# Query roots per batch on GpSimd, and the last feed-forward by halves

## The reference, cut to what matters

```python
q = (hidden @ Wq + bq).reshape(b, s, 16, 128).transpose(0, 2, 1, 3)
q = q * rsqrt(mean(q * q, -1) + 1e-6)      # the query norm; k likewise
scores = einsum('bhsd,bhed->bhse', q, k) / sqrt(128)
x = layernorm(x + (softmax(scores) @ v) @ Wo)
# gated feed-forward; _qdot casts both operands to fp8 and gives bf16
x = layernorm(x + _qdot(gelu(_qdot(x, w_gating[0])) * _qdot(x, w_gating[1]), w_linear))
```

## Time and profile before

| | |
|---|---|
| median of 3 runs | 837.78 us (837.47 to 840.25) |
| profiled execution | 837.24 us |
| span of its instructions | 835.2 us |
| mean granted clock of TensorE | 0.996 |
| PE busy | 796.5 us (95%) |
| DVE busy | 650.1 us (78%) |
| ACT busy | 528.7 us (63%) |
| POOL busy | 335.6 us (40%) |
| chain that ended last | PE 76%, DVE 10%, ACT 7%, issue 2%, POOL 2% |

### The profile page before, as it was taken

The page is one execution under the profiler, slowest core; times in us unless marked ns, Lnnn a source line. Parts: engine busy times, 40 slices in busy tenths (PEclk is TensorE's granted clock), DMA queues, the critical chain, the costliest instruction groups (busy, mean ns, idle before and its releaser), DMA issues.

```text
span 835.2 us, 13794 instructions
## 1 busy us (share of the span) xinstructions
PE 796.5 (95%) x4554; PEld 610.9 (73%) x4554; DVE 650.1 (78%) x1696; ACT 528.7 (63%) x1315; POOL 335.6 (40%) x419
## 2 busy tenths in 40 slices
PE   6899998899999999999999999999999999999985
PEld 5564576688878777886788767887788778777763
DVE  1678778798889787988878987898879877755655
ACT  3776732773664697538863598359854588578763
POOL 0686875354256213632525313723543242112110
PEclk9999999999999999999999999999999999999998
DMA  9977311001003000200100010100110001000000
GB/s 323 344 250 249 91 64 26 0 14 26 1 2 86 4 2 0 77 0 2 38 13 17 10 60 8 62 1 0 40 51 1 1 1 51 1 13 2 1 13 25
DMA packets 40517, 41.20 MB, mean 49 GB/s; under 512 B 19072, under 2 KB 34944, under 8 KB 40064
## 3 DMA queue, kind: packets, MB, share of 16 engines
q1 hardware_dynamic: 40448, 40.33, 15.2%
HBM read 31.93 MB, written 8.39 MB: 48 GB/s over the span
## 4 chain that ended last, share of the span: by engine, by line
PE 76%; DVE 10%; ACT 7%; issue 2%; POOL 2%; DMA 1%; SPq 0%; POOLq 0%; DVEq 0%; ACTq 0%
PE bank L1376 11%; PE bank L1337 10%; PE bank L1103 6%; PE bank L1160 6%; PE bank L1355 6%; PE bank L1365 5%; PE bank L1297 5%; PE bank L1230 3%; PE bank L1161 3%; PE bank L1190 3%; PE bank L1360 3%; PE bank L1097 2%; PE bank L1343 2%; PE bank L1243 2%; PE bank L1204 2%
## 5 line engine op out<-in xcount | busy, mean ns | idle before, releaser
L1337 PE MATMUL bank<-XTE,w_xq 128*128 128x256 f32 x512 | 122.0, 381 | 2.6 <-ACT QA L721 2.1
L729 ACT ACTIVATE S<-S,mx 128x128 f32<-128x128 f32 x256 | 99.4, 394 | 28.3 <-DVE mx L1034 28.0
L1376 PE MATMUL bank<-w_xo,OX 128*128 128x256 f32 x512 | 115.9, 379 | 0.0
L1337 PEld LDWEIGHTS bank<-XTE,w_xq 128*128 128x128 f32 x512 | 94.4, 190 | 20.4 <-issue 4.3
L1376 PEld LDWEIGHTS bank<-w_xo,OX 128*128 128x128 f32 x512 | 95.3, 190 | 12.2 <-issue 0.2
L1031 DVE SCALAR_TENSOR_TENSOR S<-bank,rq,xmask 128x128 f32<-128x128 f32 x256 | 71.6, 342 | 23.9 <-PE bank L1355 19.9
L720 ACT ACTIVATE QS<-bank,per_partition_sb 128x256 f32<-128x256 f32 x128 | 60.9, 475 | 28.4 <-PE bank L1337 28.2
L1160 PE MATMUL bank<-prod,taps_sb 128*128 128x256 f32 x256 | 77.6, 385 | 0.3 <-DVE Zc L846 0.3
L1355 PEld LDWEIGHTS bank<-KTX,QA 128*128 128x128 f32 x512 | 62.7, 191 | 11.5 <-issue 7.5
L1355 PE MATMUL bank<-KTX,QA 128*128 128x128 f32 x512 | 67.8, 279 | 2.2 <-ACT QA L721 1.7
L315 POOL TENSOR_TENSOR prod<-XTA,ccolA 128x256 f32<-128x256 f32 x96 | 59.1, 648 | 25.4 <-DVE prod L315 14.4
(11 more groups left out here) (230 smaller groups left out, 1744.3 us busy)
## 6 DMA issues: line engine op xcount, KB each, us to landing
keys_spilled<-KTX SPq DMA_DIRECT2D x6, 512.0 KB, 2.9
values_spilled<-VX SPq DMA_DIRECT2D x6, 512.0 KB, 4.1
KTX<-keys_spilled SPq DMA_DIRECT2D x6, 512.0 KB, 3.8
VX<-values_spilled SPq DMA_DIRECT2D x6, 512.0 KB, 4.7
xin<-in_x SPq DMA_DIRECT2D x8, 256.0 KB, 3.0
taps_sb<-in_taps SPq DMA_DIRECT2D x1, 2048.0 KB, 13.4
cnat<-in_ctx SPq DMA_DIRECT2D x8, 256.0 KB, 2.8
ccolA<-in_ctxT SPq DMA_DIRECT2D x32, 64.0 KB, 2.7
```

Source lines behind the costliest of these rows:

```text
L729: ins = nc.scalar.activation(S[:, b, seq(h)], S[:, b, seq(h)], ACT.Exp, bias=mx[:, b, h:h + 1], accum_out=sm[:, b, h:h + 1])
L1337: ins = nc.tensor.matmul(cols(EQ)[:, h], w_xq[:, k, hh * XDIM:(hh + 1) * XDIM], XTE[:, k], start=k == 0, stop=k == HALVES - 1)
L1376: ins = nc.tensor.matmul(rows(EY)[:, b], OX[:, h, b], w_xo[:, n * XGROUP + h], start=n == 0 and h == 0 and b == 0, stop=n == XKV - 1 and h ...
```

## The change

Two things. POOL's `queries` calls `inverse_root` once for each batch, on four columns, with a signal for each; DVE's `scores` of batch b waits for the signal of its own batch. And group 7's feed-forward becomes a program of its own, `last_ffn`: gelu, product, transposes, cast to fp8 and the last matmuls go by halves of 512 columns, with the results in other banks; DVE takes one of the four gate copies; and the norm's output of group 6 moves on DVE from before group 7's value copies to after its last product. The strings of PE, DVE and ACT get 2, 3 and 1 more letters a at their ends; POOL's is unchanged.

```diff
 # gpsimd, queries
-                sig(inverse_root(rq[:, n % 2], sums, XDIM * 1e-6, vq[:, n % 2]), "e_rq")
+                for b in range(GB):
+                    part = slice(b * XGROUP, (b + 1) * XGROUP)
+                    sig(inverse_root(rq[:, n % 2, part], sums[:, part], XDIM * 1e-6, vq[:, n % 2, part]), "e_rq")
 # vector, queries and scores
-                    dve.wait_ge(sems["e_rq"], g * XKV + n)
+                    dve.wait_ge(sems["e_rq"], GB * (g * XKV + n))
-                    dve.wait_ge(sems["e_rq"], nth(g, XKV, n))
+                    dve.wait_ge(sems["e_rq"], nth(g, GB * XKV, GB * n + b))
 # scalar, last_ffn
+                def gate(j):
+                    half = G16[:, j // 2, j % 2 * BANK:(j % 2 + 1) * BANK]
+                    if j < 3:
+                        act.wait_ge(sems["f_gf"], nth(g, 2 * GB, j))
+                        sig(nc.scalar.activation(half, ffn_banks(g, j)[0][:], ACT.Copy), "f_g16")
+                    act.wait_ge(sems["f_g16"], nth(g, 2 * GB, j))
+                    sig(nc.scalar.activation(half, half, ACT.Gelu_apprx_tanh), "f_ga")
+
+                def turned(j):
+                    b, nh = j // 2, j % 2
+                    act.wait_ge(sems["f_aT"], last_half(j))
+                    settled(act)
+                    sig(nc.scalar.activation(A8T[:, b, 4 * nh:4 * nh + 4].rearrange("p k s -> p (k s)"),
+                                             as_bf(ffn_banks(g, j)[0])[:, 0:BANK], ACT.Copy, saturate=False), "f_a8")
...
+                for j in range(3):
+                    yield
+                    gate(j)
+                yield
+                turned(0)
+                yield
+                gate(3)
+                for j in range(1, 4):
+                    yield
+                    turned(j)
 # vector: ffn writes its norm only for groups below 6; last_ffn
+                for j in range(2):
+                    yield
+                    value(j)
+                yield
+                product(0)
+                yield
+                value(2)
+                yield
+                product(1)
+                yield
+                dve.wait_ge(sems["f_gf"], nth(g, 2 * GB, 3))
+                dve.wait_ge(sems["f_g16"], nth(g, 2 * GB, 2))
+                sig(nc.vector.tensor_copy(G16[:, 1, BANK:2 * BANK], ffn_banks(g, 3)[0][:]), "f_g16")
+                yield
+                value(3)
+                for j in range(2, 4):
+                    yield
+                    product(j)
+                yield
+                normalised(g - 1)
...
 # tensor, last_ffn: the gating matmuls are those of ffn
+                def turned(j):
+                    b, nh = j // 2, j % 2
+                    pe.wait_ge(sems["f_a"], last_half(j))
+                    for k in range(4):
+                        ins = nc.tensor.transpose(as_bf(ffn_banks(g, j)[0])[:, seq(k)], G16[:, b, seq(4 * nh + k)], ident_bf[:])
+                    sig(ins, "f_aT")
+
+                def result(b):
+                    for nh in range(2):
+                        pe.wait_ge(sems["f_a8"], last_half(2 * b + nh))
+                        settled(pe)
+                        for k in range(4 * nh, 4 * nh + 4):
+                            ins = nc.tensor.matmul(ffn_banks(g, 2 * b)[1][:, 0:DIM], A8T[:, b, k], w_ln[:, k], start=k == 0, stop=k == FFN_K - 1)
+                    sig(ins, "f_y")
+                for j in range(3):
+                    yield
+                    turned(j)
+                yield
+                result(0)
+                yield
+                turned(3)
+                yield
+                result(1)
```

More of the change, by code:

```diff
@@ L263, in station_a @@
                     yield from ffn(g - AHEAD + 1)
-            for g in range(GROUPS - AHEAD + 1, GROUPS):
+            for g in range(GROUPS - AHEAD + 1, GROUPS - 1):
                 yield from ffn(g)
+            yield from last_ffn(GROUPS - 1)
         def each_group(program):
@@ L631, in ffn @@
                     sig(nc.scalar.activation(half, ffn_banks(g, j)[0][:], ACT.Copy), "f_g16")
[L632 to L636, removed]
                 yield
-                for b in range(GB if g < GROUPS - 1 else 0):
+                for b in range(GB):
                     act.wait_ge(sems["f_g16"], nth(g, 2 * GB, 2 * b + 1))
@@ L878, in ffn, with normalised, last_ffn, value @@
                     sig(nc.vector.tensor_tensor(UA[:, b], x[:, b], Y16[:, b], ALU.add), "f_yu")
-                    if g == GROUPS - 1 and b == 0:
+                dve.wait_ge(sems["f_yu"], nth(g, GB, GB - 1))
+                norm("f", UA)
+                if g < GROUPS - 2:
+                    yield
+                    normalised(g)
+            def normalised(g):
+                dve.wait_ge(sems["nf_rstd"], nth(g))
+                norm_out("f", UA, X[g % XBUF])
+            def last_ffn(g):
+                x = X[g % XBUF]
+                def value(j):
+                    dve.wait_ge(sems["f_gf"], nth(g, 2 * GB, j))
+                    sig(nc.vector.tensor_copy(F16[:, j // 2, j % 2 * BANK:(j % 2 + 1) * BANK], ffn_banks(g, j)[1][:]), "f_f16")
+                def product(j):
+                    half = G16[:, j // 2, j % 2 * BANK:(j % 2 + 1) * BANK]
+                    dve.wait_ge(sems["f_f16"], nth(g, 2 * GB, j))
+                    dve.wait_ge(sems["f_ga"], last_half(j))
+                    sig(nc.vector.tensor_tensor(half, half, F16[:, j // 2, j % 2 * BANK:(j % 2 + 1) * BANK], ALU.mult), "f_a")
+                for j in range(2):
[18 more added lines that the diff above has]
+                normalised(g - 1)
+                for b in range(GB):
+                    yield
+                    dve.wait_ge(sems["f_y"], nth(g, GB, b))
+                    order(nc.vector.tensor_copy(Y16[:, b], ffn_banks(g, 2 * b)[1][:, 0:DIM]))
+                    sig(nc.vector.tensor_tensor(UA[:, b], x[:, b], Y16[:, b], ALU.add), "f_yu")
+                    if b == 0:
                         dve.wait_ge(sems["f_yu"], nth(g, GB, 0))
@@ L882, in ffn @@
                 dve.wait_ge(sems["f_yu"], nth(g, GB, GB - 1))
[L883 removed]
+                norm("f", UA, GB - 1)
                 yield
[L885 to L886 removed]
+                normalised(g)
             def ternary_ffn(g):
@@ L1049, in output @@
                 norm_out("e", UE, x)
-            together(ORDER["dve"], s=set_up(), a=station_a(front, ffn), c=station_c(ternary_ffn, recurrent), r=recurrent(0), k=station_k(keys, no_turning), q=station_q(queries),
+            together(ORDER["dve"], s=set_up(), a=station_a(front, ffn, last_ffn), c=station_c(ternary_ffn, recurrent), r=recurrent(0), k=station_k(keys, no_turning), q=station_q(queries),
                      x=each_group(lambda g: scores(g, 0)), y=each_group(lambda g: scores(g, 1)), o=each_group(output))
@@ L1205, in ffn, with last_ffn @@
                     sig(ins, "f_y")
+            def last_ffn(g):
+                yield from ffn(g)
+                def turned(j):
[14 more added lines that the diff above has]
+                    turned(j)
+                yield
+                result(0)
+                yield
+                turned(3)
+                yield
+                result(1)
             def ternary_ffn(g):
```

23 lines of the change are left out of this document (16 added, 7 removed).

## The result

The kernel after takes 841.70 us (median of 6 runs, 840.48 to 843.9), the kernel before 837.62 beside it on the same chip (6 runs, 836.9 to 840.25): a ratio of 1.0053, 95% interval 1.0041 to 1.0065. It is slower by 4.1 us by the medians, by 4.4 by the ratio (3.4 to 5.4). The forecast was 839.6 us with a range up to 841.5; the sign is right, the size is less than half of what came, and the time lies outside the range.

The account below looks back on a forecast made before the run. TensorE was taken to bound most of 200 to 800 us, a chain of waits the end after 808. Profiled 837.24 + 2.63 of stalls - 0.8 = 839.1, on the median 839.6 us; range 836.8 to 841.5, forecast's own 838.4 to 840.8.

Parts of the forecast that it names:

- 155, 411 and 741: DVE's waits at 154.98, 411.30 and 741.04: earlier or later roots there change nothing for TensorE, each priced at 0.
- The tail: Last feed-forward by halves: DVE reads the last result at 828.0 instead of 828.79, 0.8 us gained, bounds 0.2 and 1.2.
- rival (a): Query roots on POOL: four columns cost what eight cost, 6.9 us slower in all, 844.7 us; chance 0.06.
- The queue behind the other roots: POOL's queue behind roots not listed: users come later than 0.8 us or a gap comes first, so no stall.
- at 375: DVE waits for batch 1's root at 368.86; the chain to X, which TensorE turns at 374.87, stalls 0.73 us.
- At 258: Four POOL products behind the root, used by TensorE at 258.56: 0.82 late less 0.06 slack, 0.76 us stall.
- At 450: POOL products ended at 450.00, used by TensorE at 450.40: 0.82 late less 0.40 slack, 0.42 us stall.
- At 183: DVE's convolution products behind batch 1's root, taken by TensorE at 183.02: 0.82 less 0.10 slack, 0.72 us stall.
- (b): Delays priced at 0, at 741.04 and 411.30, reach TensorE too: 2 x 0.8 us more, 841.2 us; chance 0.15.
- (c): Stalls in the middle of the run get absorbed, only the last feed-forward's gain is left: 837.0 us; chance 0.25.
- (d): Last feed-forward gives nothing, since DVE with its thirteen steps becomes the bound: 840.4 us; chance 0.06.
- (e): The clock: a fall of the clock costs 1.3 us; chance 0.06.

Follow-up runs that it names:

- the roots alone: Kernel before with the split roots but its old last feed-forward: 843.57 us, ratio 1.0074 to the kernel before.
- the tail alone: Kernel after with the whole roots of before, so only the new last feed-forward is changed: 836.14 us, ratio 0.9984 to the kernel before.
- the queue alone: Kernel before, roots whole, plus an unused four-column addition and power on POOL behind each root: 845.40 us, ratio 1.0096 to the kernel before.
- the norm first: Whole roots and new last feed-forward, but DVE writes group 6's norm ahead of group 7's value copies again: 836.50 us, ratio 0.9995 to before.
- the addition on VectorE by halves: Whole-root kernel with new last feed-forward, changed: DVE adds the root's small constant, POOL takes the power per batch, four columns twice: 839.4 us, ratio 1.0035 to before.
- the run without the addition: Whole roots and new last feed-forward, but query roots omit adding the small constant, leaving out part of the computation: 833.03 us, ratio 0.9958 to before.

## Why the prediction missed, step by step

**Right.** A root of four columns: forecast 1.04 on a straight line between two and eight columns, measured 1.038. POOL's extra: some 25 us, measured 25.4. That the trace is to be read by who stands directly behind a root, that the stalls add where TensorE is the bound (5.85 in the trace, 6.2 in the time), and that three places swallow theirs: 155, 411 and 741 came as said. The tail: 0.94 gained in the trace (1.26 between traces without a fall of the clock there) and 1.3 us by the ratio (0.3 to 2.3), where 0.8 was forecast. For the power the rows say about 0.4 us fixed and 0.16 us a column (0.72, 1.04, 1.67 for two, four, eight), so rival (a) is dead. The Trainium skill (GPSIMD Engine Reference, section 3.1) gives about 2.6 cycles an element for an addition of two tensors, and 4497 ns for 2048 elements a partition, by which I estimate 2.2 ns each; that doesn't carry over to the power's 160 ns a column.

**The step that failed** is the sentence "The queue behind the other roots leads to users later than 0.8 us, or meets a gap of POOL's first". I looked behind each root for the products and the norms, and for DVE's own waits for the roots. Four things were there that I did not look for:
- srms of the ternary feed-forward, queued right behind root 10 (386): 0.87. Its slack was 0.04, so the rule that I used would have given 0.78 there had I listed it.
- The same behind root 3 (228): 0.73. Here listing it would not have been enough: the slack was 0.71 on DVE, and the 0.82 of the forecast less that is only 0.11. The second half took 0.73 and 1.32 beside other work of DVE's, and the pair took 3.79 where the root of before took 2.21.
- The wait on the transpose of the sums. In before it is no idle time in any view, since the root had ended 0.16 earlier; it stands only in the code, at L1022. 0.51 at 690.
- A second consumer at 375: the softmax's normalisation in DVE's order behind the late score. I followed one chain to X and stopped: 1.04 instead of 0.73, so 0.31.

That is 2.42 of the 3.41 us by which the stalls (6.04) exceed the sum (2.63). **The other 0.99 is sizes.** At 258, 0.39: the second addition took 0.55 and not 0.25, beside other work of DVE's, so the pair took 3.11 and not 2.82. At 450, 0.48: the slack of 0.40 was read in rows where the products took 2.38; 0.8 later they run beside other work of DVE's and take 2.83. A slack is measured with one neighbour, and whoever is shifted gets another. At 183, 0.12.

**The rivals.** (b) said that delays priced at 0 reach TensorE too, 841.2 us. Its time is nearly the one measured, but at places that it names, 741 and 411, nothing was lost; the loss was at places that no case named. (c), all absorbed, is refuted by the roots alone, (d) by the tail alone. (a) is refuted by the tile's row. (e), the clock: see below; its 1.3 us for a fall is the upper end of what the traces show, and it didn't decide the result. That (b) came so near in time is luck. The range failed for the same cause as the sum: it was made of the places that I knew, and had no term for a place that I had missed, while seven of 32 roots turned out to matter and I had four of them. The forecast's own bounds are also mis-summed: a root of 0.9 with the tail's 1.2 gives 838.1 by the prediction's own terms, and one of 1.15 with the tail's 0.2 gives 841.1, not 838.4 and 840.8. The measured 841.7 is outside both.

## What to carry to other kernels

Before a step on a side engine is made longer, list for each of its instances the next two or three entries of that engine's queue and every wait in the code on its signal (not only those that show idle time), and compare each reader's slack with the lateness. Here 25 of 32 places were free and seven cost some 6 us, so a split is worth having only where its first half is waited for, and can be applied to single instances. And a slack of a few tenths is not a number to subtract: after the shift, the instruction that had it runs beside another neighbour.

## What the runs showed of the hardware

**Neighbours on DVE.** Of the 128 additions and powers of the query roots in after, 22 took clearly longer than their like without any wait shown: additions 0.39 to 0.74 us instead of 0.23, powers 1.3 to 1.5 instead of 1.04. Beside each of them ran one of six DVE instructions that read SBUF: the normalisation of S, the product of X and g, the one with dscaleT, the product of G and F, a norm's output or the scaling of H. These six were picked from the rows themselves; other DVE instructions that read SBUF, maxima and statistics for instance, ran beside additions and powers that kept their length. At 224.90 and 225.71 it is the product of X and g, which took 1.28; at 259.05 it is the scaling of H. At 455 four products took 2.83 instead of 2.38, beside the product with dscaleT, 1.15. Of the 106 others 23 ran beside such an instruction for over 0.1 us and kept their length. So this is a coincidence in time, though a strong one (22 of 45 against none of 83), and no run took the neighbour away. The Trainium skill (GPSIMD Engine Reference, section 1) says that this engine shares its SBUF interfaces with VectorE, with contention when a DVE instruction has two SBUF inputs or a two-port mode. The rows are in line with it, but the trace doesn't tell in which mode the norms' outputs and the scaling of H ran, which have one such input, nor why 23 kept their length. Weighed in the prediction it would have widened the lateness from 0.8 to 1.1 and more at 228 and 258, and the products at 450.

**The clock.** I compared the tail of all twelve profiles. After, by windows (us, busy us and instructions of each engine, then the clock):

```profile
core 0: us, PE busy (x) PEld busy (x) DVE busy (x) ACT busy (x) POOL busy (x), PEclk, DMA share, GB/s
815.00:820.00 5.00, 4.39 (x26) 3.44 (x24) 2.24 (x4) 3.97 (x5) 0.00 (x0) 1.00 0.01 3
820.00:825.00 5.00, 3.47 (x22) 2.68 (x23) 2.91 (x9) 1.97 (x2) 1.18 (x2) 0.68 0.00 0
```

The clock of 0.68, so in part 1.2 GHz, stands ahead of the last feed-forward, as the 0.71 of before does. From ScalarE's last fp8 copy of group 6 to its fp8 copy of the last input pass 3.65 us here and 3.89 in before, and 3.7 to 3.9 in five experiments; without a fall of the clock it takes 2.76, in five others. Some of that is hidden again: the last feed-forward of the old form takes 8.60 behind such a fall and 8.92 without it. In two of those five the clock falls inside the last feed-forward instead: 9.99 us with the roots alone, where the queue alone has 8.92, and 9.82 with the norm first, where a new tail takes 7.66 and the norm's place adds 0.85. So one fall costs some 0.8 to 1.3 us in the tail, and nine of twelve executions paid for one there; the tail alone, the queue alone and the addition on VectorE by halves did not. Two experiments had another one behind TensorE's gap at 386 (1.0 to 1.2 us), and after and the run without the addition had one at 71 us (1.3 us), behind a gap of TensorE's of some 2.0 us where before has 1.44. The Trainium skill (TensorE: Matmul & The Clock Gate, Part 1) says that the gate's phase against the kernel differs from run to run; that kernels with the same instructions in the tail differ in this agrees with it. So two single profiles can differ by 1 us for this alone, and smaller differences are to be read from medians or from shifts between one place and the next.
